# Top-k attention as a difference of exponentials, with keys and scores made two batches ahead

## The chip, the cores and the metric

One core of a Trainium2 chip runs the whole program. The metric is the device time of one execution in microseconds; three runs of the kernel before are shown. The engines are PE (matrix multiply, with PEld for its weight loads), DVE (vector), ACT (activation), POOL (GpSimd) and SP, whose queue issues the DMAs. Each works its own instructions in order and waits on semaphores for the others.

## The reference, cut to what matters

Six blocks follow one another (a state-space scan, cross attention, a mixture of experts, a four-layer encoder, the block of this change, and a coupling network), each added to its input and normalised. The change lies in the fifth, with B = 16 batches, T = 112 rows, 375 context rows (of 192 features) and H = 4 heads of 32, of whose scores K_TOP = 32 per row are kept:

```python
Q = (x_text @ Wq).reshape(Bb, Tt, H, DH)
K = (x_vision @ Wk).reshape(Bb, Gg, H, DH)
scores = jnp.einsum('bthd,bghd->bhtg', Q, K) / np.sqrt(DH).astype(np.float32)
scores = jnp.where(vision_mask[:, None, None, :], scores, -jnp.inf)
topv, topi = jax.lax.top_k(scores, K_TOP)
probs = jax.nn.softmax(topv, axis=-1)
attn = jnp.zeros_like(scores).at[bi, hi, ti, topi].set(probs)
attn_mean = attn.mean(axis=1)
V = x_vision @ Wv
c_t = jnp.einsum('btg,bgd->btd', attn_mean, V)
c_t = c_t * text_mask[..., None]
```

`c_t` then scales and shifts (FiLM) the normalised rows ahead of a long convolution, which needs all sixteen batches.

## The kernel before

The stage runs over 16 batches b and 4 heads h; n = 4b + h counts heads. Scores of head h lie in PSUM bank h. Four more banks (4 to 7) are a ring for everything else PE makes: `m_uses` writes out by hand in which order keys ("k"), attention ("at"), gathered context ("m1"), values ("ct"), queries and turned rows take them, and `m_claim` makes PE wait until the use four before has been copied out by ACT.

*SP* (`s4x_load`, L2022 and L2026): for each batch `ctx_k`, the context row by row, and `ctx_f`, the same by features. Each has two buffers; `ctx_f` of b waits for the keys of b-2, `ctx_k` of b for the gather of b-2. Behind batch 1 SP also asks for the next weights (L2030) and the first six groups of convolution taps (L2033).

*PE* (`s4x_pe`): in turn b it makes the keys of b+1 (`topk_keys`, L2073), four heads' scores of b+1 (`scores`: L2110 for q times k and L2112, which adds the mask), then `attend(b)` (L2121, 24 recorded matmuls: each head's exponentials times a diagonal matrix `dg` of its reciprocal sum, summed over heads), `gather(b)` (L2132) and, behind every fourth batch, `values` (L2141).

*DVE* (`s4x_dve`): two heads at a time. MAX8 (L2359) finds a row's eight largest, MATCH_REPLACE8 (L2368) writes the row to `w_s` with these replaced by FILL = -3e38; four rounds make the 32. Behind the first MAX8 `neg_m` (L2363) takes the negative maximum. Then a SCALAR_TENSOR_TENSOR (L2378) multiplies ACT's exponentials `e_p` by (w_s == FILL) and sums them into `e_sum`; after the fourth head a reciprocal (L2381) and a scale by text mask and 1/4 (L2382) give `e_rs`. `w_s` and `top8` have one buffer for each head of a pair.

*ACT* (`s4x_act`): per head e_p = exp(score - max) from PSUM (L2308), and at h = 1 the copies of the batch before: attention to `at_t` (L2277), context to `m1` (L2282, L2283), values to `c_t` (L2287), keys to `k_e` (L2274). At a batch's end it builds `dg` (L2317). In batch 0, ahead of head 2, it copies all eight pairs of turned rows with their sums (L2294, L2295).

*POOL* (`s4x_pool`): once these sums are there it works the norms of all 16 batches' rows (L2458 to L2474), and is idle in the rest of the stage. At the stage's end PE takes the FiLM products (`film`, L2168) of the first batches between `attend(15)`, `gather(15)` and the last values, and DVE's `modulate` uses them.

## Time and profile before

| What | Value |
|---|---|
| Time, three runs | 2377.91, 2368.76, 2375.60 us; median 2375.6 |
| The profiled execution's own time | 2369.8 us |
| Its span, first to last instruction | 2368.0 us |
| Mean granted clock of TensorE in it | 0.895 |
| Share of the span, busy | PE 89%, DVE 64%, ACT 30%, POOL 34% |
| The stage of the change | about 1700 to 2030 us |

The span and the time differ by 1.8 us, which lies around the instructions. A busy share is over the whole span and thus over stages with different limits; the rows further below are of the one stage. Windows are given in microseconds from the span's start, durations of single instructions in nanoseconds. The granted clock is a share of 2.4 GHz, and 0.50 is 1.2 GHz.

### The profile page before, as it was taken

How to read it: one execution, taken by the hardware profiler on the slowest of the kernel's cores; microseconds unless marked ns; L12 is line 12 of the kernel's file. 1: busy time of each engine (PE TensorE's matmuls, PEld its weight loads, DVE VectorE, ACT ScalarE, POOL GpSimd, SP SyncE). 2: the span in 40 equal slices, each digit the busy share in tenths (PEclk: the TensorE clock that was granted, in tenths of full speed). 3: DMA queues.
4: the chain of work that ended last, by engine and by line, in shares of the span. 5: the costliest groups of instructions: out<-in, count | busy, mean ns of one | idle time of the engine just before them, and what ended most of it. 6: DMA issues, size and time to landing. Idle time of an engine off the chain costs nothing.

```text
span 2368.0 us, 37754 instructions
## 1 busy us (share of the span) xinstructions
PE 2104.5 (89%) x15300; PEld 1469.8 (62%) x15300; DVE 1514.5 (64%) x3047; ACT 712.4 (30%) x1407; POOL 810.7 (34%) x726
## 2 busy tenths in 40 slices
PE   7988879999999978999999999999767777979986
PEld 2324347777766656888888888887445555436632
DVE  7998955566333324555565555676498998637546
ACT  6445324333312112222322223232232222111132
POOL 3242448967600005444444444442270000013101
PEclk9768689999799989999999999999865766989998
DMA  5222183222010017201000100100321110310001
GB/s 156 73 73 90 57 162 93 64 67 69 10 54 0 1 48 198 58 2 65 6 1 1 70 2 1 52 2 1 110 62 30 30 30 25 103 35 1 0 0 31
DMA packets 67181, 114.47 MB, mean 48 GB/s; under 512 B 34153, under 2 KB 58722, under 8 KB 65794
## 3 DMA queue, kind: packets, MB, share of 16 engines
q1 hardware_dynamic: 67010, 112.07, 16.4%
q8 instruction: 122, 2.00, 0.4%
q14 instruction: 49, 0.40, 0.1%
HBM read 91.56 MB, written 33.34 MB: 53 GB/s over the span
## 4 chain that ended last, share of the span: by engine, by line
PE 66%; DVE 23%; POOL 5%; issue 3%; ACT 2%; DMA 0%; DVEq 0%; SPq 0%; POOLq 0%; ACTq 0%
PE PS L1535 8%; PE PS L1551 8%; PE PS L1280 5%; PE PS L1258 4%; DVE top L2359 4%; DVE w_s L2368 4%; PE PS L1448 2%; PE PS L2239 2%; PE PS L2229 2%; PE PS L1510 2%; PE PS L892 2%; PE PS L1462 2%; PE PS L2168 2%; PE PS L1562 2%; PE PS L879 2%
## 5 line engine op out<-in xcount | busy, mean ns | idle before, releaser
L289 POOL TENSOR_SCALAR ln_ve<-ln_mv 128x2 f32<-128x2 f32 (+1 forms) x87 | 20.2, 232 | 1186.4 <-DVE ln_mv L273 1186.3
L1832 POOL TENSOR_TENSOR q_x<-q_f,cols 128x2048 f32<-128x2048 f32 x56 | 217.8, 3911 | 9.3 <-ACT q_f L1652 7.5
L1782 DVE TENSOR_TENSOR p_x<-PS,cols 128x1024 f32<-128x1024 f32 x112 | 129.2, 1216 | 123.9 <-PE PS L1497 123.9
L1089 DVE TENSOR_REDUCE XD<-PS 112x2 f32<-112x750 f32 x128 | 119.9, 939 | 93.1 <-PE PS L879 92.6
L457 PE MATMUL PS<-bc_parts,ident 96*128 96x448 bf16 x256 | 107.4, 525 | 40.6 <-DVE st_h L691 26.8
L1048 ACT ACTIVATE e_t<-PS 125x672 f32<-125x672 f32 x128 | 93.6, 731 | 155.8 <-PE PS L892 155.8
L1337 DVE SCALAR_TENSOR_TENSOR XA<-PS,gate_w,XA 112x256 f32<-112x256 f32 x128 | 56.0, 479 | 125.7 <-PE PS L1280 125.7
L2121 PE MATMUL PS<-dg,e_p 112*125 112x112 f32 x384 | 79.6, 399 | 60.8 <-ACT dg L2317 60.8
L879 PE MATMUL PS<-enc_w,q_s 32*112 32x375 f32 x512 | 130.7, 534 | 1.9 <-DVE XD L1089 1.9
L1639 ACT ACTIVATE wb<-PS,cols 128x256 f32<-128x256 f32 x224 | 91.0, 473 | 134.9 <-PE PS L1535 134.9
L892 PE MATMUL PS<-q_s,enc_w 32*125 32x112 f32 x1536 | 123.5, 292 | 2.2 <-ACT e_t L1048 2.2
L2121 PEld LDWEIGHTS PS<-dg,e_p 112*125 112x125 f32 x384 | 76.4, 311 | 74.3 <-issue 74.3
L647 DVE TENSOR_TENSOR_SCAN st_h<-dA,st_h 128x3584 f32<-128x3584 f32 x16 | 121.0, 7606 | 0.0
L1280 PE MATMUL PS<-wc,q_s 128*112 128x256 f32 x512 | 116.0, 380 | 0.3
L746 POOL TENSOR_TENSOR st_h<-st_h 128x448 f32<-128x448 f32 x64 | 71.3, 1136 | 109.9 <-DVE st_h L691 109.9
L892 PEld LDWEIGHTS PS<-q_s,enc_w 32*125 32x125 f32 x1536 | 102.4, 192 | 7.9 <-issue 7.9
L1280 PEld LDWEIGHTS PS<-wc,q_s 128*112 128x112 f32 x512 | 89.7, 177 | 26.9 <-issue 9.2
L1535 PE MATMUL PS<-wc 128*128 128x256 f32 x448 | 103.7, 391 | 1.4 <-ACT wc L1681 1.4
L1258 PE MATMUL PS<-XF,wc 128*128 128x448 f32 x256 | 101.6, 540 | 0.0
L2368 DVE MATCH_REPLACE8 w_s<-top,w_s 112x375 f32<-112x375 f32 x192 | 100.9, 532 | 0.0
L1551 PE MATMUL PS<-enc_w,wb 128*128 128x256 f32 x448 | 99.0, 379 | 0.0
L1551 PE MATMUL PS<-wc,wb 128*128 128x256 f32 x448 | 99.0, 379 | 0.0
(366 smaller groups left out, 4704.6 us busy)
## 6 DMA issues: line engine op xcount, KB each, us to landing
k_full_scratch<-k_scratch SPq DMA_DIRECT2D x112, 112.0 KB, 2.9
v_all_scratch<-v_st SPq DMA_DIRECT2D x16, 750.0 KB
v_t<-v_all_scratch SPq DMA_DIRECT2D x16, 750.0 KB
t_ring<-k_full_scratch SPq DMA_DIRECT2D x8, 784.0 KB, 12.7
enc_w<-in_enc_w SPq DMA_DIRECT2D x2, 3072.0 KB, 11.2
wc<-in_enc_w SPq DMA_DIRECT2D x2, 3072.0 KB, 12.1
k_all_scratch<-k_st SPq DMA_DIRECT2D x16, 375.0 KB
enc_w<-k_all_scratch SPq DMA_DIRECT2D x64, 93.8 KB, 3.6
```

The lines of the kernel that those rows point to most:

```text
L647: dve.tensor_tensor_scan(h, dA[:, n, :, :].rearrange("p n b t -> p (n b t)"), h, 0.0, ALU.mult, ALU.add).then_inc(scan_done, 1)
L879: ins = pe.matmul(ps[2 * (n % 2) + a][0:T, 0:S2], q_s[h, m, b * T:(b + 1) * T], k_s[h, b % 3, m, :], start=True, stop=True)
L892: ins = pe.matmul(ps[4 + a][0:JR, j * T:(j + 1) * T], k_s[h, b % 3, m, j * JR:(j + 1) * JR], q_s[h, m, b * T:(b + 1) * T], start=True, sto ...
L1089: dve.tensor_reduce(nm_w[0:T, g % 4, 64 * half + 16:64 * half + 49:32], PS[0:T, 2 * half:2 * half + 2, 0:S2], AX.X, ALU.max, negate=True). ...
L1258: last = pe.matmul(ps[pair + m][:, 0:QT], w1_e[:, e, k, m * P:(m + 1) * P], XF[:, k, q * QT:(q + 1) * QT], start=(k == 0), stop=(k == KC - 1))
L1280: last = pe.matmul(bank, h_t[:, i % 2, k, b * T:(b + 1) * T], w2_e[:, e, k, :], start=(k == 0), stop=(k == KC - 1))
L1535: last = pe.matmul(ps[bank][:, (m % 2) * RT:(m % 2 + 1) * RT], w[:, k, m * P:(m + 1) * P], x1f[:, i % 2, k, :], start=(k == 0), stop=(k == ...
L1551: last = pe.matmul(ps[3][:, g * D:(g + 1) * D], h_ff[:, m, g * P:(g + 1) * P], w[:, m, :], start=(m == 0), stop=(m == 7))
L1782: last = dve.tensor_tensor(p_x[:, m, :, :, :], ps[1][:, m * P:(m + 1) * P].rearrange("p (h i) -> p h i", i=16).unsqueeze(2) .to_broadcast( ...
L1832: last = pool.tensor_tensor(q_x[:, c, :, :].rearrange("p t (h i) -> p t h i", i=16), q_f[:, k % 2, c, :].rearrange("p (t i) -> p t i", i=1 ...
L2121: last = pe.matmul(bank[0:JR, j * T:(j + 1) * T], e_p[:, XH * (b % 2) + h, j * JR:(j + 1) * JR], dg[:, b % 2, h, :], start=(h == 0), stop= ...
L2368: ins = dve.match_replace(w_s[:, a, :], top8[:, a, turn, :], s, FILL)
```

## The change

What it does, by engine:

- *DVE*: the multiply and sum, the reciprocal and its scale go. `w_s` and `top8` get a buffer for each of the four heads. The first MAX8 of a head waits for `x_rest` of the same head a batch ago, its first replace for `x_cut`. After the stage DVE waits for `attend(14)` before it writes `x2`.
- *ACT*: `rest_and_sum` takes the exponential of `w_s` in place (where a score was replaced it is 0) and of the 32 kept scores with their sum. It does so for heads 0 and 1 ahead of head 2's `e_p`, for heads 2 and 3 at the batch's end. `weights` (`dg`) of b-1 comes behind the keys' copy at h = 1 of b; attention and context of b-1 are copied at h = 3, values at the end of the batch after. The turned rows are copied four pairs in batch 0 and four in batch 1.
- *POOL*: per head e_p - w_s, so that only the kept ones stay; per batch the power -1 of the sums and the scale by the text mask (now over 4). One step of the norms follows each subtraction, from batch 2 on.
- *PE*: keys and scores are made two batches ahead, scores two heads at a time, heads 2 and 3 behind the gather. The mask product has both operands in BF16.
- *SP*: the features of b+1 are asked for ahead of `ctx_k` of b.
- `at_t` lies in `wa`, whose weights are not used any more by then; the fourth block of `ident16` is filled.

The diff, cut to its core:

```diff
-        w_s = sb("w_s", [T, 2, S2], pool=s4a)
-        mskb = sb("mskb", [P, S2], pool=s4a)
+        e_p = sb("e_p", [T, 2 * XH, S2], pool=s4a)
+        w_s = sb("w_s", [T, XH, S2], pool=s4a)
+        mskb = sb("mskb", [P, S2], BF16, pool=s4a)
...
-        top8 = sb("top8", [T, 2, 4, 8], pool=s4a)
+        top8 = sb("top8", [T, XH, 4, 8], pool=s4a)
...
-        at_t = sb("at_t", [JR, 2, JC, T], pool=s4a)
+        minus = sb("minus", [T, XH], pool=s4a)
+        at_t = wa[0:JR, :, :].rearrange("p k n -> p (k n)")[:, 0:2 * JC * T].rearrange("p (z j t) -> p z j t", z=2, j=JC)
...
-            for k in range(3):
+            for k in range(4):
...
-            for b in range(B):
+
+            def load_features(b):
                 if b >= 2:
                     sp.wait_ge(m_ready, m_count("k", b - 2) + 1)
                 for i in range(2):
                     sp.dma_start(ctx_f[0:CR[i], b % 2, i, :], dr["ctxT"][b, i * P:i * P + CR[i], :])\
                         .then_inc(ctx_loaded[b % 2], 16)
+
+            load_features(0)
+            for b in range(B):
+                if b + 1 < B:
+                    load_features(b + 1)
                 if b >= 2:
                     sp.wait_ge(m_ready, m_count("m1", b - 2) + 1)
                 sp.dma_start(ctx_k[:, b % 2, :, :], dr["ctx"][b].rearrange("(j p) f -> p j f", p=JR))\
...
-                if 1 <= b < B - 1:
-                    uses.append(("k", b + 1))
+                if b + 2 < B:
+                    uses.append(("k", b + 2))
...
-            def scores(b):
+            def scores(b, heads):
                 pe.wait_ge(m_used, max(m_count("k", b), m_count("q", b // QB)) + 1)
-                for h in range(XH):
+                for h in heads:
                     n = XH * b + h
                     if n >= 4:
                         pe.wait_ge(x_exp, n - 3)
                     r = slice(32 * h, 32 * h + 32)
                     pe.matmul(ps[h][0:T, 0:S2], q_e[r, b * T:(b + 1) * T], k_e[r, b % 2, :],
                               start=True, stop=False)
-                    pe.matmul(ps[h][0:T, 0:S2], ident[r, 32 * h + b:32 * h + b + 1].to_broadcast([32, T]), mskb[r, :],
+                    pe.matmul(ps[h][0:T, 0:S2], ident16[r, b:b + 1].to_broadcast([32, T]), mskb[r, :],
                               start=False, stop=True).then_inc(x_s_ready, 1)
...
-            scores(0)
+            scores(0, range(XH))
             queries(2)
             queries(3)
             topk_keys(pe, 1)
-            for j in range(B // 2):
+            scores(1, (0, 1))
+            for j in range(B // 4):
                 turn_rows(j)
-            for b in range(B):
-                if b + 1 < B:
-                    if b >= 1:
-                        topk_keys(pe, b + 1)
-                    scores(b + 1)
-                    attend(b)
-                    gather(b)
-                    if b % QB == QB - 1:
-                        values(b // QB)
+            scores(1, (2, 3))
+            for j in range(B // 4, B // 2):
+                turn_rows(j)
+            for b in range(B - 1):
+                if b + 2 < B:
+                    topk_keys(pe, b + 2)
+                    scores(b + 2, (0, 1))
+                attend(b)
+                gather(b)
+                if b + 2 < B:
+                    scores(b + 2, (2, 3))
+                if b % QB == QB - 1:
+                    values(b // QB)
...
                 act.copy(m1[0:CR[1], 1, b * T:(b + 1) * T], bank[0:CR[1], T:2 * T]).then_inc(m_used, 1)
-                if b % QB == QB - 1:
-                    q = b // QB
-                    for c in range(KC):
-                        act.copy(c_t[:, c, q * QT:(q + 1) * QT], m_bank(act, "ct", 2 * q + c)[:, 0:QT])\
-                            .then_inc(m_used, 1)
+
+            def copy_values(q):
+                for c in range(KC):
+                    act.copy(c_t[:, c, q * QT:(q + 1) * QT], m_bank(act, "ct", 2 * q + c)[:, 0:QT])\
+                        .then_inc(m_used, 1)
+
+            def rest_and_sum(b, h):
+                act.wait_ge(x_sel, XH * b + h + 1)
+                bias = neg_m[:, h:h + 1]
+                act.activation(w_s[:, h, :], w_s[:, h, :], ACT.Exp, bias=bias)
+                tops = top8[:, h, :, :].rearrange("t r v -> t (r v)")
+                act.activation(tops, tops, ACT.Exp, bias=bias, accum_out=e_sum[:, b % 2, h:h + 1])\
+                    .then_inc(x_rest, 1)
+
+            def weights(b):
+                act.wait_ge(x_rs, b + 1)
+                for h in range(XH):
+                    last = act.activation(dg[:, b % 2, h, :], ident[0:T, 0:T], ACT.Copy,
+                                          scale=e_rs[:, b % 2, h:h + 1])
+                last.then_inc(x_dg, 1)
 
...
             for b in range(B):
                 for h in range(XH):
                     n = XH * b + h
-                    if n == 2:
-                        copy_keys(1)
-                        for j in range(B // 2):
-                            copy_rows(j)
                     act.wait_ge(x_first, n + 1)
                     if b >= 2 and h == 0:
                         act.wait_ge(m_ready, m_count("at", b - 2) + 1)
                     act.activation(e_p[:, XH * (b % 2) + h, :], ps[h][0:T, 0:S2], ACT.Exp,
                                    bias=neg_m[:, h:h + 1]).then_inc(x_exp, 1)
-                    if b >= 1 and h == 1:
-                        copy_attention(b - 1)
-                        copy_context(b - 1)
-                        if b + 1 < B:
-                            copy_keys(b + 1)
-                act.wait_ge(x_rs, b + 1)
-                for h in range(XH):
-                    last = act.activation(dg[:, b % 2, h, :], ident[0:T, 0:T], ACT.Copy,
-                                          scale=e_rs[:, b % 2, h:h + 1])
-                last.then_inc(x_dg, 1)
+                    if h == 1:
+                        if b == 0:
+                            copy_keys(1)
+                        else:
+                            if b == 1:
+                                for j in range(B // 4, B // 2):
+                                    copy_rows(j)
+                            if b + 1 < B:
+                                copy_keys(b + 1)
+                            weights(b - 1)
+                        rest_and_sum(b, 0)
+                        rest_and_sum(b, 1)
+                    elif h == 3:
+                        if b == 0:
+                            for j in range(B // 4):
+                                copy_rows(j)
+                        else:
+                            copy_attention(b - 1)
+                        rest_and_sum(b, 2)
+                        rest_and_sum(b, 3)
+                        if b >= 1:
+                            copy_context(b - 1)
+                            if b % QB == 0:
+                                copy_values(b // QB - 1)
+            weights(B - 1)
             copy_attention(B - 1)
             copy_context(B - 1)
+            copy_values(NQ - 1)
             for j in range(TAPS):
...
                         for a, h, n in pair:
                             if turn == 0:
                                 dve.wait_ge(x_s_ready, n + 1)
+                                if b >= 1:
+                                    dve.wait_ge(x_rest, n - 3)
                             elif turn == 1:
                                 dve.wait_ge(x_first, n + 1)
                             else:
                                 link.after(cut[a])
-                            s = ps[h][0:T, 0:S2] if turn == 0 else w_s[:, a, :]
-                            found[a] = link.mark(dve.max(top8[:, a, turn, :], s))
+                            s = ps[h][0:T, 0:S2] if turn == 0 else w_s[:, h, :]
+                            found[a] = link.mark(dve.max(top8[:, h, turn, :], s))
                         if turn == 0:
                             for a, h, n in pair:
                                 link.after(found[a])
-                                found[a] = link.mark(dve.tensor_scalar(neg_m[:, h:h + 1], top8[:, a, 0, 0:1], -1.0,
+                                found[a] = link.mark(dve.tensor_scalar(neg_m[:, h:h + 1], top8[:, h, 0, 0:1], -1.0,
                                                                        None, ALU.mult))
                         for a, h, n in pair:
                             link.after(found[a])
-                            s = ps[h][0:T, 0:S2] if turn == 0 else w_s[:, a, :]
-                            ins = dve.match_replace(w_s[:, a, :], top8[:, a, turn, :], s, FILL)
+                            if turn == 0 and b >= 1:
+                                dve.wait_ge(x_cut, n - 3)
+                            s = ps[h][0:T, 0:S2] if turn == 0 else w_s[:, h, :]
+                            ins = dve.match_replace(w_s[:, h, :], top8[:, h, turn, :], s, FILL)
                             if turn == 0:
                                 ins.then_inc(x_first, 1)
+                            elif turn == 3:
+                                ins.then_inc(x_sel, 1)
                             else:
                                 cut[a] = link.mark(ins)
-
-                    for a, h, n in pair:
-                        link.after(cut[a])
-                        dve.wait_ge(x_exp, n + 1)
-                        e = e_p[:, XH * (b % 2) + h, :]
-                        last = link.mark(dve.scalar_tensor_tensor(e, w_s[:, a, :], FILL, e, ALU.is_equal, ALU.mult,
-                                                                  accum_out=e_sum[:, b % 2, h:h + 1]))
-                    link.after(last)
-                link(dve.reciprocal(e_rs[:, b % 2, :], e_sum[:, b % 2, :]))
-                dve.tensor_scalar(e_rs[:, b % 2, :], e_rs[:, b % 2, :], tmk[:, b:b + 1], 1.0 / XH,
-                                  ALU.mult, ALU.mult).then_inc(x_rs, 1)
...
+                if b == 0:
+                    dve.wait_ge(m_ready, m_count("at", B - 2) + 1)
...
+            def norm_row(b):
+                if b == 0:
+                    pool.wait_ge(m_used, m_count("x", B // 2 - 1) + 1)
+                    link(pool.tensor_scalar(row_mean, row_sum, 1.0 / D, None, ALU.mult))
+                    link(pool.tensor_tensor(row_sum, row_mean, row_mean, ALU.mult))
+                    link(pool.tensor_scalar(row_sq, row_sq, 1.0 / D, EPS, ALU.mult, ALU.add))
+                    link(pool.tensor_tensor(row_sq, row_sq, row_sum, ALU.subtract))
+                    link(pool.tensor_tensor(row_rs.rearrange("t (q i) -> t q i", i=QB),
+                                            row_sq.rearrange("t (q i) -> t q i", i=QB),
+                                            halves[0:T, :].unsqueeze(1).to_broadcast([T, NQ, QB]), ALU.pow))
+                g, i = XN_AT[b]
+                link(pool.tensor_scalar(xn_rows[g][:, i, :], XA[0:T, b, :], row_mean[:, b:b + 1],
+                                        row_rs[:, b:b + 1], ALU.subtract, ALU.mult))
+
+            def norm_scale(g):
+                x = xn_rows[g]
+                n = sum(a == g for a, i in XN_AT)
+                link(pool.tensor_tensor(x, x, e_row4("g_in")[:, 0:n, :], ALU.mult))
+
+            def norm_shift(g):
+                x = xn_rows[g]
+                n = sum(a == g for a, i in XN_AT)
+                pool.tensor_tensor(x, x, e_row4("b_in")[:, 0:n, :], ALU.add).then_inc(x2_affine, 1)
+
             for b in range(B):
-                g, i = XN_AT[b]
-                last = pool.tensor_scalar(xn_rows[g][:, i, :], XA[0:T, b, :], row_mean[:, b:b + 1],
-                                          row_rs[:, b:b + 1], ALU.subtract, ALU.mult)
-                n = i + 1
-                if b == B - 1 or XN_AT[b + 1][0] > g:
-                    link(last)
-                    x = xn_rows[g]
-                    link(pool.tensor_tensor(x, x, e_row4("g_in")[:, 0:n, :], ALU.mult))
-                    pool.tensor_tensor(x, x, e_row4("b_in")[:, 0:n, :], ALU.add).then_inc(x2_affine, 1)
+                for h in range(XH):
+                    n = XH * b + h
+                    pool.wait_ge(x_rest, n + 1)
+                    e = e_p[:, XH * (b % 2) + h, :]
+                    pool.tensor_tensor(e, e, w_s[:, h, :], ALU.subtract).then_inc(x_cut, 1)
+                    if h == XH - 1:
+                        link(pool.tensor_tensor(e_rs[:, b % 2, :], e_sum[:, b % 2, :], minus[:, :], ALU.pow))
+                        pool.tensor_scalar(e_rs[:, b % 2, :], e_rs[:, b % 2, :], tmk[:, b:b + 1], None,
+                                           ALU.mult).then_inc(x_rs, 1)
+                    if XH * 2 <= n < XH * 2 + B:
+                        norm_row(n - XH * 2)
+                    elif XH * 2 + B <= n < XH * 2 + B + 10:
+                        g, half = divmod(n - XH * 2 - B, 2)
+                        if half == 0:
+                            norm_scale(g)
+                        else:
+                            norm_shift(g)
```

## Rows read from the trace of the kernel before

**Rows 1.** The page: busy time of each engine, and the chain by line

```profile
PE 2104.5 (89%) x15300; PEld 1469.8 (62%) x15300; DVE 1514.5 (64%) x3047; ACT 712.4 (30%) x1407; POOL 810.7 (34%) x726
...
PE PS L1535 8%; PE PS L1551 8%; PE PS L1280 5%; PE PS L1258 4%; DVE top L2359 4%; DVE w_s L2368 4%; PE PS L1448 2%; PE PS L2239 2%; PE PS L2229 2%; PE PS L1510 2%; PE PS L892 2%; PE PS L1462 2%; PE PS L2168 2%; PE PS L1562 2%; PE PS L879 2%
```

**Rows 2.** Stretches: length, PE, PEld, DVE, ACT, POOL busy, granted clock, DMA share, GB/s

```profile
1706.56:2022.17 315.61, 227.42 (x913) 155.72 (x912) 300.94 (x993) 87.85 (x256) 47.78 (x35) 0.66 0.15 42
1942.40:1967.00 24.60, 21.45 (x63) 12.95 (x64) 18.45 (x64) 6.47 (x17) 0.00 (x0) 0.50 0.09 24
```

**Rows 3.** DVE's timeline, one undisturbed batch: start us, us, what

```profile
1850.37 1.01 DVE L2359 MAX8 top<-PS 112x8 f32<-112x375 f32 x2
...
1858.34 0.54 DVE L2378 SCALAR_TENSOR_TENSOR e_p<-w_s,e_p 112x375 f32<-112x375 f32 x1
...
1859.39 1.01 DVE L2359 MAX8 top<-PS 112x8 f32<-112x375 f32 x2
...
1867.37 0.54 DVE L2378 SCALAR_TENSOR_TENSOR e_p<-w_s,e_p 112x375 f32<-112x375 f32 x1
...
1868.77 1.00 DVE L2359 MAX8 top<-PS 112x8 f32<-112x375 f32 x2
```

**Rows 4.** Waits in 1700 to 2030 us: total us, times, longest

```profile
DVE e_p L2378 <- ACT e_p L2308: 11.3, 3, 5.2
```

**Rows 5.** DVE's timeline where the stage lost time, idle before in brackets

```profile
1733.92 2.53 DVE L2378 SCALAR_TENSOR_TENSOR e_p<-w_s,e_p 112x375 f32<-112x375 f32 x1
...
1811.22 0.55 DVE L2378 SCALAR_TENSOR_TENSOR e_p<-w_s,e_p 112x375 f32<-112x375 f32 x1 [5.20 <-ACT e_p L2308]
...
1813.57 1.01 DVE L2359 MAX8 top<-PS 112x8 f32<-112x375 f32 x2 [0.84 <-PE PS L2112]
```

**Rows 6.** DVE's groups in 1728.77 to 1769.7 us, POOL busy throughout: busy, mean ns

```profile
L2368 DVE MATCH_REPLACE8 w_s<-top,w_s 112x375 f32<-112x375 f32 x24 | 12.6, 533 | 0.0
L2378 DVE SCALAR_TENSOR_TENSOR e_p<-w_s,e_p 112x375 f32<-112x375 f32 x8 | 11.8, 1514 | 0.0
...
L2363 DVE TENSOR_SCALAR neg_m<-top 112x1 f32<-112x1 f32 x6 | 0.8, 143 | 0.0
```

**Rows 7.** PE's timeline: behind batch 11, and two score heads of batch 2

```profile
1943.83 5.35 PE L2121 MATMUL PS<-dg,e_p 112*125 112x112 f32 x24 [6.46 <-ACT dg L2317]
1949.76 2.90 PE L2132 MATMUL PS<-at_t,ctx_k 125*128 125x112 f32 x12 [0.57 <-ACT at_t L2277]
1953.24 7.20 PE L2141 MATMUL PS<-XD,enc_w 128*128 128x448 f32 x8 [0.57 <-ACT XD L2283]
1960.37 3.16 PE L2073 MATMUL PS<-ctx_f,enc_w 128*128 128x375 f32 x4
...
1741.49 2.11 PE L2110 MATMUL PS<-k_e,q_e 32*112 32x375 f32 x4 [3.11 <-ACT e_p L2308]
1742.87 1.98 PE L2112 MATMUL PS<-mskb,ident 32*112 32x375 f32 x4
```

**Rows 8.** Groups of ACT and POOL over the span: busy, mean ns

```profile
L2308 ACT ACTIVATE e_p<-PS,neg_m 112x375 f32<-112x375 f32 x64 | 34.6, 577 | 13.6 <-DVE w_s L2368 13.4
...
L290 POOL TENSOR_TENSOR ln_rs<-ln_ve,halves 112x4 f32<-112x4 f32 x24 | 25.5, 1063 | 2.0
...
L1964 POOL TENSOR_TENSOR XD<-XD 128x512 f32<-128x512 f32 x14 | 17.7, 1265 | 1.1
```

**Rows 9.** POOL's timeline at the norms before

```profile
1724.13 0.26 POOL L2458 TENSOR_SCALAR ln_st<-ln_st 112x16 f32<-112x16 f32 x1 [13.90 <-ACT PS L2295]
...
1728.77 4.85 POOL L2467 TENSOR_SCALAR XF<-XA,ln_st 112x256 f32<-112x256 f32 x4
```

**Rows 10.** The timeline at the stage's end

```profile
2020.77 0.54 DVE L2378 SCALAR_TENSOR_TENSOR e_p<-w_s,e_p 112x375 f32<-112x375 f32 x1
...
2022.29 1.22 ACT L2317 ACTIVATE dg<-ident,e_rs 112x112 f32<-112x112 f32 x4 [6.65 <-DVE e_rs L2382]
...
2023.66 2.84 PE L2121 MATMUL PS<-dg,e_p 112*125 112x112 f32 x24 [1.27 <-ACT dg L2317]
```

More of the change, by code:

```diff
@@ L1818, in enc_pool @@
                 if k == STEPS + 1:
-                    topk_masks(pool)
+                    topk_masks(pool, link)
                 if 0 <= k - 3 < STEPS - ROUNDS:
@@ L2082, in topk_masks @@
             pool.tensor_scalar(mskb[:, :], msk8[:, :], -1.0, -FAR, ALU.add, ALU.mult).then_inc(e_prep, 1)
-            pool.tensor_scalar(tmk[:, :], tmk8[:, :], 1.0, None, ALU.mult).then_inc(e_prep, 1)
+            pool.tensor_scalar(tmk[:, :], tmk8[:, :], 1.0 / XH, None, ALU.mult).then_inc(e_prep, 1)
+            link(pool.memset(minus[:, :], -1.0))
         def s4x_pe(pe):
```

15 lines of the change are left out of this document (3 added, 12 removed).

## The prediction

> **What bounds the kernel now.** I read the page first: PE is busy 89% of the span and DVE 64%, but the chain by line has DVE's top-k lines L2359 and L2368 at 4% each, two of the few entries that are not PE's [rows 1]. Such a share says nothing yet; it belongs to one stage, and there the question is which wait ends last. The stage is the one in which the change lies: from DVE's first MAX8 at 1706.56 us to the last reciprocal's scale at 2022.17, 315.6 us, DVE busy 300.9 of them, PE 227.4, ACT 87.9, POOL 47.8, granted clock 0.66 [rows 2]. So DVE sets the pace and the others follow.
>
> Next, DVE's timeline for one undisturbed batch [rows 3]: from one first MAX8 to the next batch's is 18.40 us. Two heads' selection takes 7.97 (1850.37 to 1858.34) and 7.98 (1859.39 to 1867.37); between lie the masked multiply and sum of the pair (1.05) and, after the second pair, the same with the reciprocal and its scale (1.40). Sixteen such batches are 294.4 us. The stage is 21.2 longer, and three views say where that goes. The waits: DVE sat before the multiply at L2378 for 11.3 us, three times, until ACT's exponential [rows 4]. The timeline shows two of these, 5.20 us, each followed by 0.84 for the scores [rows 5]: they lie behind batches 3 and 11, where PE's in-order queue holds the values product ahead of the next keys and scores. The third is 0.9. The last part is in the groups of 1728.77 to 1769.7: eight multiplies take 1514 ns each, where an undisturbed one takes 540 [rows 3, 6]. That is 7.8 us, and the single one of 2.53 [rows 5] shows the form: it waits while POOL runs. Together 11.3 + 1.7 + 7.8 = 20.8.
>
> **The change, part by part.** *DVE's selection.* Per batch 1.05 + 1.40 = 2.45 leaves DVE, and nothing is added but waits on x_rest and x_cut, which cost nothing once met. That leaves 15.95 per batch, 255.2 for sixteen.
>
> *ACT.* Per head one exponential of 375 elements in SBUF and one of 32 with a sum. The first is taken as the one from PSUM, 0.58 [rows 8]; the second is not in the trace, between nothing and another 0.58; I take 0.9 for the two with the read of the sum, ends 0.6 and 1.2. ACT then works some 8.5 us per batch, under 15.95, so this is hidden as long as it is not held up.
>
> *POOL.* Per head a subtraction of 375 elements. The nearest form, 512 wide, takes 1265 ns, which is 0.93 in proportion [rows 8]; I take 1.0, ends 0.9 and 1.3. Per batch one four-wide power of 1063 ns [rows 8] and its scale, some 0.26 like the small operation of [rows 9]. Without the norms 5.3 us per batch. One norm row is 1.21 (4.85 for four [rows 9]); one follows each subtraction for batches 2 to 5, and a scale or shift of four rows, about 2.4, for batches 6 to 8. The fullest batch is then 4 x 3.4 + 1.3 = 15 us, just under the 15.95.
>
> *The loop between engines.* Let selection of batch b start at 0. Heads 0 and 1 end at 8, ACT frees them at 9.3, POOL at 10.3 to 13; DVE wants their buffers again at 17.2. The second pair ends at 16, is free at 17.3, subtracted at 18.3 to 20.8, and e_rs comes at 19.6 to 22.2. ACT builds dg by 21.4, PE attends until 26.8 at the low clock (5.35 [rows 7]), ACT can copy at 28 behind the exponentials of batch b+1, the gather takes 2.90, and the last two heads' scores of b+2 are there at about 32.8, wanted by DVE at 40. The first two heads' scores of b+2 are there at 21.5, wanted at 32. So there are 7 to 10 us of slack in a plain batch.
>
> *One stall at the head.* In batch 2 POOL does its row statistics between the subtractions of heads 0 and 1: 4.64 from the first of them to the first norm row (1724.13 to 1728.77) and one row of 1.21 [rows 9]. Head 0's subtraction ends about 13.6 after the batch's start, so head 1's is done at 20.4, and DVE wants that buffer at 17.7: 2.7 us, once.
>
> *The quarters' ends.* The two stalls of now (12.1 with the scores' part) go, since keys and scores are two batches ahead. But PE now has values behind batch 3, 7 and 11 released only after ACT's rest of batch b+1's second pair, at 33.6. At the low clock it takes 7.20 and the keys 3.16 [rows 7]: 44. ACT stands in order behind it, copies keys at 44.6, weights of b+1 to 45.8, and frees head 0 and 1 of b+2 at 46.7 and 47.6, against 48 when DVE wants them; POOL's norm work behind batches 3 and 7 and the last heads' scores come 0.3 to 1.5 late. I put 1.1 for each, 3.3 in all; at full clock nothing. What is late next after a stall is thus ACT's rest, not the scores. Stalls sum to 2.7 + 3.3 = 6.0.
>
> *The masks.* The mask product becomes BF16 against BF16; two heads with both products in f32 take 3.4 us at the low clock (1741.49 to 1744.85 [rows 7]). I take 1.9 for two heads, ends 1.5 and 3.4. Only PE's queue gains.
>
> *DMAs.* SP asks for the features of b+1 ahead of ctx_k of b. The features of b+2 are then asked for a whole batch ahead of their keys, so SP's wait for the gather is no longer behind them. For batch 2 they also go ahead of the taps. Nothing to pay; without this order keys would wait on a gather. The fourth 32x32 copy of the identity and the memset of minus are each some 0.1 us in places not watched.
>
> *The end.* Now: selection ends 2020.77, dg starts at 2022.29, the last attend at 2023.66, 2.89 later [rows 10]. After: ACT's rest of both last heads +1.3, subtraction +2.3, power and scale with hand-overs +3.8, dg 1.35, attend at +5.15. From there to the end I leave all as it is.
>
> *The sum.* The last attend starts now 2023.66 - 1706.56 = 317.1 after the first MAX8; after the change 255.2 + 6.0 + 5.15 = 266.4. That is 50.7 less. The profiled execution took 2369.8, so 2319.1. The runs shown lie between 2368.8 and 2377.9 with their median 5.8 above that execution; I forecast 2322, half of that added.
>
> **A rule against the change.** In the 40 us in which POOL worked without a break, DVE's one-column neg_m took 143 ns and the replaces 533 [rows 6], as elsewhere; only the multiply with two tensors waited. The Trainium skill (SBUF — State Buffer, Who interferes with whom) agrees on the multiply, but also says that a tensor_scalar can take the pair of ports that DVE shares with GpSimd, where its operands meet the conditions, and then blocks fully behind a running GpSimd instruction. Neg_m is a tensor_scalar. By that rule its waits would have to be added; by the row nothing is. Its mechanism is priced below.
>
> **The rivals.** *All hidden* (0.10): PE at full clock and the head's stall filled, no stalls at all: 2369.8 - 56.7 = 2313. For it: the clock is granted in parts of the stage. Against: the clock was 0.50 in all of 1942 to 1967 though PE was busy 21.45 of 24.6 [rows 2].
>
> *The quarter stalls stay* (0.15): ACT in order behind the copies of values costs 6.04 at each of three ends [rows 5], 18.1 instead of 3.3: 2334. For it: ACT now has twice the work behind the same copies. Against: the wait is then in the rest, which has more room.
>
> *PE at the low clock becomes the bound* (0.05): attend 5.35, copy gap 0.57, gather 2.90, two heads 1.9, keys 3.16, gap 0.57, two heads 1.9 make 16.4 with 0.2 of hand-overs 16.6; a fourth of values with its wait for ACT (7.20 + 1.6) is 2.2: 18.8 per batch. 16 x 18.8 + 2.7 + 5.15 = 308.7, 8.4 less than now: 2361. For it: the low clock above. [...]
>
> *The same loop, with dearer scores, is slower than before* (0.03): its place is PE's queue with scores two heads at a time. If the mask's BF16 saves nothing, each pair costs 3.4, 3.0 more per batch: 21.8 x 16 + 7.85 = 356.7, 39.6 more than now, 2409. It decides from 19.3 per batch ((317.1 - 7.85) / 16). Against: it needs the low clock without a break.
>
> *Neg_m behind POOL* (0.03): POOL would work 64 x 1.0 + 16 x 1.3 + 45 for the norms, 130 of 266 us, so half of the 32 pairs would meet an operation with some 0.7 left: 11 us, 2330. The six of [rows 6] speak against it.
>
> *That the change does not do what it says*: that the multiply is still on DVE in another form. The diff shows no DVE instruction in its place, so it has no chance of its own.
>
> **How the numbers follow.** The forecast itself has 0.64. Its own range is 2313 to 2330: stalls 2.7 to 9, the unseen prices, the spread of the runs. The low end of my range is the rival with no stalls less 5 for the bounds, 2308; the high end is the quarter rival and the 8 by which the highest run lies above the profiled execution, 2342. What is left out is the two rivals of PE's loop, 0.08, and some 0.1 of the others. A measurement here tells about 0.5%, 12 us, from no change. Faster: 0.64 + 0.10 + 0.15 + 0.03 = 0.92. Same: the PE bound, 0.05. Slower: 0.03.
>
> **What would show it.** Right: in the changed profile the first MAX8s of successive batches stand 15.95 apart; MAX8 and replace keep 537 and 533 ns; no DVE wait on PE in the stage; a single DVE wait for POOL of 2 to 3 us in batch 3; the last attend 5.2 behind the last replace. Wrong: batches further apart with DVE waiting for ACT's exponentials (an ACT held up by copies of values) or for POOL; score matmuls of a pair over 3 us; neg_m over 0.2; or an end of the stage moved by less than the selection's.

## The result and the profile after

| | Before | After |
|---|---|---|
| Median of four runs | 2372.8 us (2368.8 to 2377.9) | 2314.9 us (2312.9 to 2318.5) |
| Span of the profiled execution | 2368.0 us | 2316.2 us |

The ratio is 0.976, its 95% interval 0.974 to 0.978. Forecast were 2322, between 2308 and 2342. The profiled execution of after is its slowest run, 2318.45.

The page of after, busy time and the chain by line, against [rows 1]:

```profile
PE 2090.8 (90%) x15236; PEld 1451.5 (63%) x15236; DVE 1472.7 (64%) x2888; ACT 761.1 (33%) x1599; POOL 891.5 (38%) x823
...
PE PS L1536 9%; PE PS L1552 8%; PE PS L1281 5%; PE PS L1259 4%; DVE w_s L2412 4%; DVE top L2401 3%; PE PS L1449 3%; PE PS L2252 2%; PE PS L1511 2%; PE PS L2242 2%; PE PS L2181 2%; PE PS L1563 2%; PE PS L1463 2%; PE PS L893 2%; PE PS L880 2%
```

DVE lost 42 us of work, ACT gained 49 and POOL 81. The page shows no bound that changed hands; DVE's two selection lines are still in the chain. The stage must be read alone. From its first MAX8 to the last attend, in the columns of [rows 2]:

```profile
1705.61:1969.27 263.66, 217.77 (x853) 138.09 (x853) 257.18 (x835) 137.82 (x452) 128.27 (x132) 0.66 0.19 51
```

DVE is busy 257 of 263.7 us. Before, the same stretch took 317.1; 53.4 went here, 50.7 were forecast. Behind it the profiled execution of after is 2.6 longer than before's (346.9 against 344.3 to the end of the span), in the convolution and what follows. Where that comes from was not traced: the change touches only a wait of DVE there, and the other three spans of after are 3 to 5 shorter than the profiled one.

DVE's timeline of after: the first MAX8s of two successive batches, and each place in the stage where it waited once the selection ran:

```profile
1721.55 1.01 DVE L2401 MAX8 top<-PS 112x8 f32<-112x375 f32 x2
...
1737.51 1.00 DVE L2401 MAX8 top<-PS 112x8 f32<-112x375 f32 x2
...
1803.37 0.09 DVE L2412 MATCH_VALUE_LOAD w_s<-top,PS 112x8 f32 x1 [0.28 <-POOL e_p L2523]
...
1810.56 1.01 DVE L2401 MAX8 top<-PS 112x8 f32<-112x375 f32 x2 [0.76 <-PE PS L2120]
...
1820.67 0.09 DVE L2412 MATCH_VALUE_LOAD w_s<-top,PS 112x8 f32 x1 [0.39 <-POOL e_p L2523]
...
1939.96 1.01 DVE L2401 MAX8 top<-PS 112x8 f32<-112x375 f32 x2 [1.14 <-PE PS L2120]
```

A batch takes 15.96. The four waits sum to 2.57. The two for PE are the second pairs of batches 6 and 14, whose scores PE makes after the values of batches 3 and 11; the two for POOL fall in its norm work. The same comes from the waits by releaser, where 8.8 of the 10.7 in the group's row below is the start of the stage. The groups of 1705 to 1970 us, busy and mean ns, against [rows 6, 8]:

```profile
L2401 DVE MAX8 top<-w_s 112x8 f32<-112x375 f32 x192 | 95.2, 538 | 0.0
...
L2523 POOL TENSOR_TENSOR e_p<-e_p,w_s 112x375 f32<-112x375 f32 x64 | 62.0, 982 | 131.5 <-ACT top L2308 130.4
...
L2306 ACT ACTIVATE w_s<-w_s,neg_m 112x375 f32<-112x375 f32 x64 | 38.6, 603 | 37.5 <-DVE w_s L2412 37.5
...
L2401 DVE MAX8 top<-PS 112x8 f32<-112x375 f32 x64 | 32.1, 544 | 10.7 <-PE PS L2120 10.7
L2308 ACT ACTIVATE top<-top,neg_m 112x32 f32<-112x32 f32 x64 | 19.9, 310 | 0.0
L2525 POOL TENSOR_TENSOR e_rs<-e_sum,minus 112x4 f32<-112x4 f32 x16 | 16.6, 1037 | 0.0
...
L2308 ACT ACTIVATION_READ_ACCUMULATOR top<-top,neg_m 112x1 f32 x64 | 12.2, 191 | 0.0
L2405 DVE TENSOR_SCALAR neg_m<-top 112x1 f32<-112x1 f32 x64 | 8.7, 144 | 0.0
```

POOL's 131 us and ACT's 38 of idle time in front of the new work say that both wait for DVE's selection: what moved is covered, but for DVE's two short waits for POOL.

### The profile page after: what moved, and what is told of

Same layout as the page of the kernel before. It is cut to its first block, busy times and chain, and to the rows that moved or that the text cites. A ratio compares the mean times of both kernels' runs of the same rounds, so it can differ in the third digit from the quotient of the medians.

```text
span 2316.2 us, 37833 instructions
## 1 busy us (share of the span) xinstructions
PE 2090.8 (90%) x15236; PEld 1451.5 (63%) x15236; DVE 1472.7 (64%) x2888; ACT 761.1 (33%) x1599; POOL 891.5 (38%) x823
## 4 chain that ended last, share of the span: by engine, by line
PE 68%; DVE 21%; POOL 6%; issue 2%; ACT 2%; DMA 0%; DVEq 0%; SPq 0%; POOLq 0%; ACTq 0%
PE PS L1536 9%; PE PS L1552 8%; PE PS L1281 5%; PE PS L1259 4%; DVE w_s L2412 4%; DVE top L2401 3%; PE PS L1449 3%; PE PS L2252 2%; PE PS L1511 2%; PE PS L2242 2%; PE PS L2181 2%; PE PS L1563 2%; PE PS L1463 2%; PE PS L893 2%; PE PS L880 2%
## 5 line engine op out<-in xcount | busy, mean ns | idle before, releaser
L2523 POOL TENSOR_TENSOR e_p<-e_p,w_s 112x375 f32<-112x375 f32 x64 | 62.0, 982 | 131.5 <-ACT top L2308 130.4
L1536 PE MATMUL PS<-wc,enc_w 128*128 128x256 f32 x448 | 99.0, 379 | 0.0
```

The source lines that it names most:

```text
L1536: last = pe.matmul(ps[bank][:, (m % 2) * RT:(m % 2 + 1) * RT], w[:, k, m * P:(m + 1) * P], x1f[:, i % 2, k, :], start=(k == 0), stop=(k == ...
```

## The experiments

Each is the changed kernel with one part undone, doubled or moved. The times of before in these comparisons have medians of 2370.7 to 2371.9 us; the changed kernel's 2314.9 is from its own comparison.

### The difference alone, with the old order of PE

```diff
-                if b + 2 < B:
-                    topk_keys(pe, b + 2)
-                    scores(b + 2, (0, 1))
+                if b >= 1:
+                    topk_keys(pe, b + 1)
+                scores(b + 1, range(XH))
                 attend(b)
                 gather(b)
-                if b + 2 < B:
-                    scores(b + 2, (2, 3))
```

and ACT's `copy_attention`, `copy_context` and `copy_values` of b-1 where they were before, at h = 1, with `weights` of b-1 ahead of them (before built `dg` at the end of batch b itself). The four buffers, the BF16 mask and SP's order stay new, so this is the old order of PE with the new chain, not the old order of everything.

> The difference of exponentials without the new order: PE makes keys and all four heads' scores of b+1 in turn b, as before, and ACT copies attention and context at h = 1 ahead of the keys. My theory: DVE has the same work as in the changed kernel, 15.95 us per batch, but at the low clock the scores of b+2 come only about 19.5 us after batch b's last replace (e_rs 3.8, dg 1.35, attend 5.35, gather 2.9, keys 3.2, copies 1.5, first scores 1.5), so DVE waits 3 to 4 us in most batches: 2365 us, 2350 to 2380, with DVE idle before the first MAX8 at PE or ACT. Rival, that shorter work on DVE is worth its 39 us in any order: 2325 to 2332.

Measured: 2398.8 us (2396.3 to 2400.6), ratio 1.011 [1.010, 1.013]: slower than the kernel before. Its waits in 1700 to 2030 us (total us, times, longest):

```profile
PE PS L2129 <- ACT dg L2308: 91.5, 14, 11.3
DVE top L2393 <- PE PS L2120: 73.6, 16, 9.0
...
ACT dg L2308 <- POOL e_rs L2518: 44.1, 13, 6.7
...
DVE w_s L2404 <- POOL e_p L2515: 14.5, 7, 4.8
```

PE waits 6.5 us in front of each attend for a chain that now goes DVE, ACT, POOL, ACT, and the scores that DVE wants stand around that attend. DVE's waits are 64.6 for PE behind the start's 9.0 and 14.5 for POOL, 79 us, where 15 x 3 to 4 was expected. The 39 us of removed DVE work are more than paid back. The place of the stall was as expected, its size was not: the time is above my range of 2350 to 2380, and on the other side of the kernel before. I had not counted POOL's late subtractions, nor all of the chain's hand-overs. Whether `dg` built at the batch's end would lose less was not tried.

### The order alone, with the multiply on DVE

```diff
-                        rest_and_sum(b, 0)
-                        rest_and_sum(b, 1)
...
+                    for a, h, n in pair:
+                        e = e_p[:, XH * (b % 2) + h, :]
+                        last = link.mark(dve.scalar_tensor_tensor(e, w_s[:, h, :], FILL, e, ALU.is_equal, ALU.mult,
+                                                                  accum_out=e_sum[:, b % 2, h:h + 1]))
```

with the reciprocal and its scale behind it, and neither subtraction nor power on POOL.

> The new order alone: the masked multiply, its sum and the reciprocal stay on DVE, POOL does only the norms, ACT has no rest. My theory: DVE keeps 18.40 us per batch and the collisions with POOL's norms (7.8 us), and loses the waits for ACT and PE behind the quarters (13 us): 2357 us, 2352 to 2361. Rival, that the order brings most of the gain: 2335 or less.

Measured: 2353.8 (2351.7 to 2358.8), ratio 0.993 [0.991, 0.994]. As expected: the stalls behind batches 3 and 11 go, the pitch stays 18.40, and the multiplies beside POOL's norms are long as in [rows 5]. So the order is worth 17 us and the difference alone costs 28, together they give 56: neither part is an independent saving. The difference shortens DVE's batch to 15.96, and the order makes PE's loop fit in it.

### SP's order as before

```diff
-            load_features(0)
             for b in range(B):
-                if b + 1 < B:
-                    load_features(b + 1)
+                load_features(b)
```

> The changed kernel with SP's order as before (features of b behind ctx_k of b-1). My theory: the features of b+2 are asked for only when the gather of b-1 is done, and the keys of b+2 then wait some 4 us per batch in front of attend; the loop of PE and ACT grows from about 16.6 to 20 us at the low clock and DVE stalls: 2350 us, 2335 to 2375. Rival, that the slack of 7 to 10 us per batch hides it: 2312 to 2318, no new DVE wait.

Measured: 2375.7 (2371.0 to 2379.7, eight runs), ratio 1.002 [1.001, 1.003]; the expected 2350 was too low, and the measured time is just above the range of 2335 to 2375. One move of a DMA's place in SP's queue takes the whole gain. The timeline of PE and SP in it:

```profile
1863.33 2.90 PE L2138 MATMUL PS<-wa,ctx_k 125*128 125x112 f32 x12 [0.57 <-ACT wa L2288]
...
1866.27 0.27 SPq L2031 DMA_DIRECT2D ctx_k<-in_ctx  x1
1866.58 1.03 SPq L2024 DMA_DIRECT2D ctx_f<-in_ctxT  x2
...
1872.59 3.14 PE L2078 MATMUL PS<-ctx_f,enc_w 128*128 128x375 f32 x4 [4.51 <-DMA ctx_f<-in_ctxT]
```

`ctx_k` waits for the gather, the features stand behind it, and the next keys start 6.0 after the features are asked for. PE waits for them 4.2 to 4.9 in each of ten turns. DVE waits for scores 22 times, 55.3 us with the start's 9.0, and for POOL 13.2: 59.5 in the stage, against 2.6 in the changed kernel. My prediction gave this order a sentence ("without this order keys would wait on a gather") and no price; its price is 61 us.

### All norms in one block on POOL

```diff
-                    if XH * 2 <= n < XH * 2 + B:
-                        norm_row(n - XH * 2)
+                    if n == XH * 2:
+                        for i in range(B):
+                            norm_row(i)
```

with the scales and shifts behind them.

> The changed kernel with POOL's norms in one block behind the subtraction of batch 2's first head instead of one step behind each. My theory: the block of some 45 us holds the next subtraction, DVE wants that buffer about 8 us later and stalls the rest, 37 us, once: 2352 us, 2345 to 2358, one DVE wait for POOL of 35 to 40 us. Rival, that the stall is made up for later: under 2325.

Measured: 2355.0 (2354.2 and 2355.7), ratio 0.993 [0.991, 0.995]. As expected, a single long wait of DVE for POOL (two of 1.13 for scores stand beside it):

```profile
1793.08 0.09 DVE L2412 MATCH_VALUE_LOAD w_s<-top,PS 112x8 f32 x1 [37.22 <-POOL e_p L2523]
```

POOL's queue is now between two selections of DVE, so how its old work is cut up is part of the change: 40 us hang on it.

### The mask in f32

```diff
-        mskb = sb("mskb", [P, S2], BF16, pool=s4a)
+        mskb = sb("mskb", [P, S2], pool=s4a)
```

and the f32 identity as the other operand.

> The changed kernel with the mask product again f32 against f32, four heads' scores as 2.11 + 1.98 us of matmuls a pair at the low clock instead of 1.60 + 0.52. My theory: a pair then costs 3.4 instead of 2.0 at the low clock and about 1.7 instead of 1.0 at full clock, so PE's loop grows by 1.4 to 2.8 us a batch. Plain batches have 7 to 10 us of slack and show nothing; behind batches 3, 7 and 11, where DVE already waited 0.76 and 1.14 us for the scores, the wait grows to 2 to 4 each. 2314.9 + 4 to 8: 2320, between 2315 and 2326. Rival (the dearer scores are the difference between a loop that holds and one that does not, by my slower-than-before mechanism): DVE waits for PE in most batches, over 2335. Rival (PE's clock rises with its added work and gives it back): 2315 or less, waits unchanged.

Measured: 2323.8 (2317.3 to 2332.0), ratio 0.980 [0.978, 0.983], 9 us over the changed kernel; the 2320 was near. A pair took 2.85 at the low clock (1.60 and 1.47, which overlap), not 3.4, so the f32 mask costs 0.9 a pair. DVE's waits for scores are 3.02, 3.02 and 2.03, at the second pairs of batches 10, 14 and 15; at batch 6 there is none, with PE granted 0.99 in 1780 to 1796 us, where the changed kernel had 0.50. A wait for POOL is there too, which I had not expected of this run: the one that the prediction had placed at the head of the stage. POOL's timeline, and the wait that it makes:

```profile
1755.17 0.98 POOL L2523 TENSOR_TENSOR e_p<-e_p,w_s 112x375 f32<-112x375 f32 x1 [7.19 <-ACT top L2308]
...
1761.71 0.98 POOL L2523 TENSOR_TENSOR e_p<-e_p,w_s 112x375 f32<-112x375 f32 x1
...
1762.79 0.09 DVE L2412 MATCH_VALUE_LOAD w_s<-top,PS 112x8 f32 x1 [3.49 <-POOL e_p L2523]
```

Batch 2 starts at 1741.27 there, so its first subtraction starts 13.9 behind it. In the changed kernel it starts at +8.6, and no such wait is seen:

```profile
1746.09 0.98 POOL L2523 TENSOR_TENSOR e_p<-e_p,w_s 112x375 f32<-112x375 f32 x1 [3.13 <-ACT top L2308]
...
1748.29 2.93 POOL L2501 TENSOR_TENSOR ln_st<-ln_st,halves 112x16 f32<-112x16 f32 x1
...
1752.64 0.98 POOL L2523 TENSOR_TENSOR e_p<-e_p,w_s 112x375 f32<-112x375 f32 x1
```

The row of 1736 to 1754 us (columns as above) gives the difference, first the changed kernel, then this one:

```profile
1736.00:1754.00 18.00, 14.65 (x87) 9.85 (x86) 18.00 (x60) 9.03 (x29) 10.60 (x13) 0.95 0.21 57
```

```profile
1736.00:1754.00 18.00, 16.86 (x60) 10.61 (x58) 17.76 (x58) 7.40 (x25) 5.14 (x6) 0.50 0.12 33
```

PE was granted 0.95 there and 0.50 here. At the low clock gather and keys are late, ACT in order behind the keys' copy is late with its rests, and POOL with its first subtraction. Against the start of batch 2 the keys of batch 3 end 5.8 later than in the changed kernel, of which the two dearer mask products ahead of them are 1.9.

### POOL's subtraction twice

```diff
-                    pool.tensor_tensor(e, e, w_s[:, h, :], ALU.subtract).then_inc(x_cut, 1)
+                    link(pool.tensor_tensor(e, e, w_s[:, h, :], ALU.subtract))
+                    pool.tensor_tensor(w_s[:, h, :], e, w_s[:, h, :], ALU.subtract).then_inc(x_cut, 1)
```

> The changed kernel with each of POOL's 64 subtractions followed by a second one of the same size (w_s = e_p - w_s, into the buffer that DVE writes next), some 1.0 us more per head with its hand-over, 4.1 per batch and 64 in all. It prices the cover over POOL. My theory: POOL's plain batch goes from 5.2 to 9.4 us and hides in 15.95; the batches with norms go from some 12 to 16 or 17, so batches 2 to 5 show DVE's first replace waiting for POOL, 1 to 3 us a batch, 4 to 10 in all; the tail from last replace to last attend grows by about 2 (two subtractions of each of the last two heads, one of each beside others). 2314.9 + 8: 2323, between 2317 and 2330. Rival (POOL's two-operand work slows DVE once it is busy half the time, as it slowed the multiply): MAX8 and replace means above 538 and 534 ns, and over 2340. Rival (all covered): 2317.

Measured: 2337.8 (2335.9 to 2338.0), ratio 0.986 [0.985, 0.987]: 23 us more, outside what I expected. The second subtraction takes 980 ns, 62.7 in all, of which some 40 stay covered. The waits of the stage:

```profile
ACT dg L2314 <- POOL e_rs L2527: 32.5, 9, 6.3
...
DVE top L2401 <- PE PS L2120: 14.5, 3, 8.8
DVE w_s L2412 <- POOL w_s L2524: 10.8, 9, 2.7
```

DVE's waits for POOL, 10.8, are about what I had put. What I had left out is the second way in which POOL counts: a late `e_rs` makes `dg`, attend and the scores behind it late (5.7 for PE behind the start's 8.8, in a row that does not name POOL), and the tail from last replace to last attend is 7.6 instead of 5.4. By its profile the stage is 281.2 long, 17.5 more, and the whole span is 17.4 more: behind the stage nothing was lost. The other 5 us of the medians are the choice of executions: the profiled one is the fastest of this kernel and was the slowest of the changed kernel. MAX8 and replace keep 538 and 534 ns with POOL busy 191 of 281 us, so no contention was seen.

### The last two heads on DVE

```diff
+            for a, h, n in pair:
+                link.after(cut[a])
+                dve.wait_ge(x_exp, n + 1)
+                e = e_p[:, XH * (b % 2) + h, :]
+                last = link.mark(dve.scalar_tensor_tensor(e, w_s[:, h, :], FILL, e, ALU.is_equal, ALU.mult,
+                                                          accum_out=e_sum[:, b % 2, h:h + 1]))
```

in batch 15 alone, with reciprocal and scale.

> The changed kernel, but the last two heads of batch 15 go the old way: masked multiply and sum, reciprocal and scale on DVE, where nothing follows them. My theory: from the last replace to the last attend 5.36 us become about 2.9 to 3.6, since ACT's two rests, POOL's subtraction and its power leave the chain for one DVE multiply, a reciprocal and a scale: the time falls by 2, to 2312.9, below what the rounds can tell; the trace decides. Rival (the film products ahead of the last attend's operands, or the gather and values behind it, hold the end anyway): the stage's end moves by under 0.5.

Measured: 2316.9 (2312.8 to 2318.2), no difference from the changed kernel. The trace decides for the rival:

```profile
1960.78 2.90 PE L2140 MATMUL PS<-wa,ctx_k 125*128 125x112 f32 x12 [0.57 <-ACT wa L2290]
1963.61 4.43 PE L2181 MATMUL PS<-enc_w,c_t 128*112 128x512 f32 x8
1967.88 2.77 PE L2129 MATMUL PS<-dg,e_p 112*125 112x112 f32 x24
```

`dg` was built from 1964.01 on, yet the last attend starts at 1967.88, behind two FiLM products, with no idle time on PE. In the changed kernel both chains end together:

```profile
1962.21 2.90 PE L2140 MATMUL PS<-wa,ctx_k 125*128 125x112 f32 x12 [0.58 <-ACT wa L2290]
1965.05 4.39 PE L2181 MATMUL PS<-enc_w,c_t 128*112 128x512 f32 x8
1969.27 2.79 PE L2129 MATMUL PS<-dg,e_p 112*125 112x112 f32 x24
```

### With the values moved behind the next turn's keys and first scores

```diff
+                if b % QB == 0 and b:
+                    values(b // QB - 1)
                 attend(b)
                 gather(b)
                 if b + 2 < B:
                     scores(b + 2, (2, 3))
-                if b % QB == QB - 1:
-                    values(b // QB)
```

with the last two heads on DVE. It ran twice, the second time beside the changed kernel.

> As the run before, and the values of batches 3, 7 and 11 on PE stand behind the keys and first two heads' scores of the next turn, their copies on ACT one pair later. My theory: the two waits of DVE for scores of 0.76 and 1.14 us behind batches 7 and 15's fourths go, as the 7.2 us of values are no longer ahead of the next keys; with the shorter end the time falls by 4 to 5 from 2314.9: 2310.5, between 2307 and 2314. Rival (values then stand ahead of the attend of the next batch, which frees ACT and POOL later): waits for POOL or ACT in place of those for PE, no gain over the run before, 2313.

> The changed kernel unaltered, beside the next one on one chip. It prices the spread: 2314.9, between 2311 and 2319. My theory of the head's stall: it comes when PE is at the low clock in batch 1 (gather 2.90 and keys 3.16 instead of 1.61 and 1.72), as in the run with the f32 mask, and not at full clock, as in the first profile; so this profile shows either both or neither. Rival: the f32 mask itself made it, then there is no wait for POOL over 1 us in batch 3 whatever the clock.

> The last two heads on DVE and the values moved, again: 3.9 us below the changed kernel beside it, as in the stage (259.75 instead of 263.66 from first MAX8 to last attend), so near 2311 and the two medians 2 to 5 apart. Rival: the gain in the stage is given back in the convolution behind it, medians within 1.

Measured: 2313.2 (2312.4 to 2318.3) and 2315.9 (2314.6 to 2316.7); the changed kernel beside the latter 2317.4 (2315.5 to 2321.9). In that comparison the ratios to before are 0.9765 [0.975, 0.978] and 0.9774 [0.976, 0.979]: 1.6 us apart where 2 to 5 were expected, not told from none. (In the text on record "behind batches 7 and 15's fourths" should be batches 3 and 11.) The wait of 1.14 went in both runs, and that of 0.76 was there in both, as 0.78 and 0.77. In the changed kernel PE stood idle ahead of the values, until ACT had copied the context, 0.31 us behind batch 3 and 3.84 behind batch 11:

```profile
1787.14 7.20 PE L2149 MATMUL PS<-XD,enc_w 128*128 128x448 f32 x8 [0.31 <-ACT XD L2296]
...
1916.54 7.20 PE L2149 MATMUL PS<-XD,enc_w 128*128 128x448 f32 x8 [3.84 <-ACT XD L2296]
```

With the values moved, the next keys fill that gap: the last two heads' scores of batch 14 start 2.5 earlier against the stage's first MAX8, those of batch 6 only 0.4. Behind batch 3 there was no gap to fill. At the low clock PE needs 23.7 us from the last two heads' scores of batch 5 to those of batch 6 (1784.92 to 1808.62) against DVE's 15.96, wherever the values stand in that turn.

The stage took 259.75 in the first, 262.79 in the second, against 263.66 and 263.79 of the changed kernel. The two differ in the clock of one stretch. PE ahead of the last attend, first run, then second:

```profile
1957.97 1.61 PE L2141 MATMUL PS<-wa,ctx_k 125*128 125x112 f32 x12 [0.57 <-ACT wa L2291]
1959.51 3.69 PE L2182 MATMUL PS<-enc_w,c_t 128*112 128x512 f32 x8
1963.03 2.77 PE L2130 MATMUL PS<-dg,e_p 112*125 112x112 f32 x24
```

```profile
1959.57 2.90 PE L2141 MATMUL PS<-wa,ctx_k 125*128 125x112 f32 x12 [0.57 <-ACT wa L2291]
1962.40 5.41 PE L2182 MATMUL PS<-enc_w,c_t 128*112 128x512 f32 x8
1967.65 2.77 PE L2130 MATMUL PS<-dg,e_p 112*125 112x112 f32 x24
```

Gather and FiLM products cost 5.3 at the one clock and 8.3 at the other. So what the edits free is there only where the clock is granted; my 2 to 5 was read from one lucky profile. Of the changed kernel's second profile, the one with `dg` as the bound of the end (PE idle 2.75 behind the FiLM products) gives the other case: the tail from last replace to last attend is 5.40 again. No version tried is shown to beat the changed kernel. On the head's stall the second profile of the changed kernel shows neither low clock (0.97 in 1736 to 1754 us) nor the wait, like the first. That agrees with the clock as its cause, but no run with the changed order of PE and POOL's subtraction had the BF16 mask and 0.50 throughout there, so it is not shown that the clock alone makes it. The f32 mask is not needed for it: the run with SP's order as before has the BF16 mask, its keys waited 4.94 for the features, its first subtraction stands 14.6 behind the start of batch 2, and DVE waited 4.52 for POOL in batch 3. So late keys made it there, with PE still at full clock for the gather ahead of them (1.61 us).

## Why the prediction was right

**DVE's selection**: 15.95 a batch forecast, 15.96 measured, MAX8 and replace unchanged. This is the term that carries the result: 16 x 2.44 = 39 of the 53.

**The new work**: ACT's rest 0.9 forecast, and the pitch of one head's two exponentials is 0.81 (603 and 310 ns overlap, then 191 for the read of the sum). POOL's subtraction 1.0, measured 0.98; the power 1.06, 1.04. Two heads' scores at the low clock 1.9, and 1.91 in the trace; the f32 pair that they replace was put at 3.4 from one place in the trace of before and took 2.85 in its own run, so that rival (scores dearer by 1.5 a pair) was overpriced. The tail 5.15, measured 5.36, but by two chains at once: besides POOL's and ACT's that I added up, PE's FiLM products ahead of the last attend end at the same time, and I had not looked at them.

**The stalls** were the step that failed: 6.0 forecast, 2.57 measured. The head's 2.7 did not come. The prediction gives the end of head 0's subtraction, 13.6 behind its batch's start (so a start at 12.6), without its terms; I had costed it with PE at the low clock up to there. PE was at full clock for batch 0's gather and batch 3's keys (1.61 and 1.72 us), and the subtraction started at 8.6. The f32-mask run, at the low clock, shows 13.9 and a wait of 3.49: the mechanism is right and its condition was not met. The quarters' 3.3 were 0.76, 0 and 1.14 for scores and 0.67 for POOL. My sentence that "what is late next after a stall is thus ACT's rest, not the scores" is wrong: PE's scores of heads 2 and 3 are late, as the sentence before it had allowed ("the last heads' scores come 0.3 to 1.5 late"), and "no DVE wait on PE in the stage" was wrong with it. The 0.76 is the price of a turn with values at the low clock, 23.7 us on PE. The turn behind batch 7 took 13.2 at a granted clock of 0.78 and nothing waited; in the changed kernel's second profile it took 22.8, and the scores were ready just as DVE wanted them.

**The rivals**: "all hidden", 2313, came closer to the median than the forecast did, though 2.6 us of stalls are there. The quarter stalls did not stay. PE did not become the bound at 0.66 granted clock. Its mechanism is real all the same: the run without the new order, by a loop through PE, was slower than before. Neg_m took 144 ns against 143 in [rows 6] with POOL busy 128 of 264 us, and still did so with POOL busy 191 of 281. The Trainium skill (SBUF — State Buffer, Who interferes with whom) has a tensor_scalar blocked behind GpSimd where its operands meet the conditions; in this form, one column in f32, no run here shows it. The kernel with the order alone shows it once for DVE's scale of `e_rs`, four columns, which took 1.97 us instead of 0.23 (rows at the end). The changed kernel has no such instruction left in the stage.

**The sum**: 317.1 to 263.7 is 53.4, of which 39 is DVE's work, 7.8 the multiplies beside POOL [rows 6], 13.0 the waits [rows 4, 5] less the new 2.6, and 2.5 comes back as the longer tail; 39.0 + 7.8 + 13.0 - 2.6 - 2.5 = 54.7. Of that 1.4 is counted twice: the multiply, reciprocal and scale of the last batch stand both in the sixteen batches and in the tail of before.

**The number** is partly luck. The profiled execution was forecast at 2319.1 and took 2318.45, but largely because the stage's 2.7 less met 2.6 more behind it. I then added 2.9 because the median of before lay above its profiled execution; the median of after lies 3.6 below its own. These two make 6.5 of the 7.1 between 2322 and 2314.9.

## What to carry to other kernels

Moving work off the bounding engine pays only if the loop through the other engines fits in the shorter batch: here the same removal made the kernel 28 us slower in the old order, and 39 us faster in the new one (2353.8 to 2314.9). Price every queue that stands between two uses of a buffer, the DMA queue's order too, which cost 61 us. Work moved within a turn of an in-order queue gains only the idle time that it fills, here 3.84 us behind batch 11 and 0.31 behind batch 3. A stall that depends on the granted clock needs two numbers, one for each level, and a chance between them.

## What the runs showed of the hardware

In the two traces that have both, DVE's masked multiply was long only beside POOL's products and sums of two large tensors. Of the eight in [rows 6] six stood beside such work and took 0.89 to 2.68, and the two beside a scaling took 0.54. In the kernel with the order alone, first DVE's and then POOL's timeline:

```profile
1753.80 0.55 DVE L2414 SCALAR_TENSOR_TENSOR e_p<-w_s,e_p 112x375 f32<-112x375 f32 x1
...
1762.37 2.52 DVE L2414 SCALAR_TENSOR_TENSOR e_p<-w_s,e_p 112x375 f32<-112x375 f32 x1
...
1767.74 1.97 DVE L2418 TENSOR_SCALAR e_rs<-e_rs,tmk 112x4 f32<-112x4 f32 x1
```

```profile
1750.04 9.36 POOL L2506 TENSOR_SCALAR XF<-XA,ln_st 112x256 f32<-112x256 f32 x7
...
1762.13 2.34 POOL L2512 TENSOR_TENSOR XF<-XF,enc_w 112x1024 f32<-112x1024 f32 x1
...
1767.05 2.64 POOL L2512 TENSOR_TENSOR XF<-XF,enc_w 112x1024 f32<-112x1024 f32 x1
```

Beside the one-tensor scaling it takes 0.55, beside the two-tensor product 2.52, which ends just behind POOL's 2.34. I had taken all of POOL's norm work as the cause. The scale of `e_rs`, one tensor of four columns, met the same once: 1.97, to the end of POOL's product, where the other fifteen took 0.23. MAX8, replace and neg_m, which read one tensor and small operands, kept their times beside POOL's subtraction of two tensors in the runs read for it.

The granted clock followed no plan that the kernel could rely on. It was 0.50 in 1780 to 1796 us of the changed kernel with PE busy 15.1 of 16.0, and the same eight FiLM matmuls took 3.69 or 5.41 in two executions of one program.
